# A decoder block on one core: scan factor, value sums and gates moved to other PSUM banks, and the orders of all engines laid anew

## What is computed

```
h = layer_norm(layernorm(x)); xk, xv, xr = mixes of h and h one token earlier
k, v = xk @ Wk.T, xv @ Wv.T;  sr = sigmoid(xr @ Wr.T)
r = sr * wkv(decay, first, k, v)        # a scan over the tokens, with a running maximum
n = layernorm(x); y = n + r @ Wo.T; h2 = layer_norm(y); xk, xr = mixes of h2
x = x + (y + sigmoid(xr @ Wrec.T) * (square(relu(xk @ Wkey.T)) @ Wval.T))
q = layernorm(x); per token: 16 heads of 16, scores q.k / 4 over the 16 heads of the
    same token of ctx, causal mask, softmax, sum over ctx's heads
x = x + that
x = x + gelu(layernorm(x) @ U1 @ V1 + b1) @ U2 @ V2 + b2
```

## Time and profile before

| | us |
|---|---|
| runs of the kernel | 1248.64, 1262.07, 1250.37; median 1250.37 |
| the profiled execution | 1249.77 |
| its span (first to last instruction) | 1247.8 |
| mean granted TensorE clock | 0.945 of full |
| busy: PE, DVE, ACT, POOL | 1032.6, 1111.0, 935.8, 867.1 |

### The profile page before, as it was taken

How to read it: one execution, slowest core, us unless ns; L and a number is a source line. 1 busy time by engine, 2 the same in 40 slices (tenths; PEclk the granted TensorE clock), 3 DMA queues, 4 the chain that set the end, 5 groups by cost and what they waited for, 6 DMA issues and landing times.

```text
span 1247.8 us, 14567 instructions
## 1 busy us (share of the span) xinstructions
PE 1032.6 (83%) x3584; PEld 584.6 (47%) x3584; DVE 1111.0 (89%) x2172; ACT 935.8 (75%) x2005; POOL 867.1 (69%) x783
## 2 busy tenths in 40 slices
PE   2679598989898989989798989989698998869515
PEld 1336263636455463736355463736346363626202
DVE  3755999999999999999999999999999999988681
ACT  4877779698888889796788879697688979464413
POOL 0112968788795968687595968688496968777680
PEclk9789799999999999999899999999899999979657
DMA  5010101001010101010010102001010101010000
GB/s 186 17 51 18 34 1 34 18 18 51 17 51 18 51 17 50 0 48 20 17 50 18 51 0 68 0 18 50 17 50 17 34 1 51 1 34 18 1 17 17
DMA packets 38964, 38.39 MB, mean 31 GB/s; under 512 B 2932, under 2 KB 38648, under 8 KB 38904
## 3 DMA queue, kind: packets, MB, share of 16 engines
q1 hardware_dynamic: 38904, 37.77, 9.5%
HBM read 29.38 MB, written 8.39 MB: 30 GB/s over the span
## 4 chain that ended last, share of the span: by engine, by line
PE 44%; DVE 32%; ACT 11%; issue 7%; POOL 4%; SPq 1%; DMA 0%; DVEq 0%; ACTq 0%; POOLq 0%
PE bank L813 19%; PE bank L870 8%; DVE x L1364 6%; PE bank L901 5%; DVE stat L1154 4%; PE bank L820 4%; PE bank L894 3%; DVE aa L1265 3%; PE bank L913 2%; DVE pp L1222 2%; POOL prod L338 2%; PE bank L885 2%; POOL prod L350 2%; DVE x L1306 2%; ACT n L462 2%
## 5 line engine op out<-in xcount | busy, mean ns | idle before, releaser
L338 POOL TENSOR_TENSOR prod<-q,kv_ctx 128x256 f32<-128x256 f32 (+5 forms) x448 | 394.7, 920 | 221.1 <-ACT q L462 221.1
L350 POOL TENSOR_TENSOR prod<-prob,v_dh 128x256 f32<-128x256 f32 (+3 forms) x256 | 390.9, 1568 | 29.2 <-ACT prob L564 29.2
L813 PE MATMUL bank<-xk,w_key 128*128 128x512 f32 x512 | 241.8, 612 | 17.6 <-DVE xk L1196 17.6
L870 PE MATMUL bank<-w_val,hidden 128*128 128x256 f32 x1024 | 225.9, 379 | 0.0
L870 PEld LDWEIGHTS bank<-w_val,hidden 128*128 128x128 f32 x1024 | 193.6, 190 | 32.4 <-issue 7.7
L1364 DVE TENSOR_REDUCE x<-prod 128x64 f32<-128x256 f32 (+3 forms) x256 | 189.9, 808 | 5.5 <-POOL prod L350 5.5
L1326 DVE TENSOR_REDUCE score<-prod 128x16 f32<-128x256 f32 (+5 forms) x448 | 175.5, 463 | 10.0 <-POOL prod L338 10.0
L813 PEld LDWEIGHTS bank<-xk,w_key 128*128 128x128 f32 x512 | 94.5, 194 | 141.8 <-issue 127.4
L548 ACT ACTIVATE hidden<-bank 128x512 f32<-128x512 f32 x128 | 74.9, 585 | 66.8 <-PE bank L813 66.7
L827 PE MATMUL bank<-ident,n 128*128 128x128 f32 x384 | 61.7, 297 | 75.5 <-ACT n L462 75.5
L422 ACT ACTIVATE lnv<-mv,eps_col 128x4 f32<-128x4 f32 x64 | 18.4, 287 | 127.2 <-DVE mv L1161 127.2
(11 more groups left out here) (96 smaller groups left out, 1946.4 us busy)
## 6 DMA issues: line engine op xcount, KB each, us to landing
x_in<-in_x SPq DMA_DIRECT2D x16, 512.0 KB, 3.6
kv_ctx<-in_ctx SPq DMA_DIRECT2D x16, 512.0 KB, 3.7
n<-in_x SPq DMA_DIRECT2D x16, 512.0 KB, 3.5
out<-y_out SPq DMA_DIRECT2D x16, 512.0 KB, 4.5
w_key<-in_wkey SPq DMA_DIRECT2D x1, 1024.0 KB
w_val<-in_wval SPq DMA_DIRECT2D x1, 1024.0 KB
w_k<-in_wk SPq DMA_DIRECT2D x1, 256.0 KB, 3.8
w_v<-in_wv SPq DMA_DIRECT2D x1, 256.0 KB, 4.2
```

The lines of the kernel that those rows point to most:

```text
L338: ins = pool.tensor_tensor(o, a, b, ALU.mult)
L350: ins = pool.tensor_tensor(o, ph[:, HB * n:HB * n + HB, 0:keys].unsqueeze(2).to_broadcast(shape), vh[:, :, 0:keys].unsqueeze(1).to_broadca ...
L813: mm = pe.matmul(to[:, :], w[:, fi, P * f:P * f + P], src[:, fi, :], start=(fi == 0), stop=(fi == CH - 1))
L870: mm = pe.matmul(bank[6 + t // 2][:, C * (t % 2):C * (t % 2) + C], hidden[:, j, P * t:P * t + P], w_val[:, j, :], start=(j == 0), stop=(j ...
```

## The change

1. The factor e1 isn't a tile any more: `split_rise` and `exp_e1` write it into bank f over k, and both scans read it there. So `project_r(f)`, whose output goes to bank f, waits for `aa_done` of half 0 and `bb_done` of half 1.
2. `sum_values` writes bank 5, `over_mass` works in bank 5, `third_residual` reads bank 5 and writes x3. The two halves s share the bank: `sum_values` for t = 0 waits for x3 of the group before, for t = 2 for the first half's x3.
3. `project_rec`, `gate_of_rec`, `transpose_4` and `copy_n4T` use bank 4 for both halves, one after the other.
4. `ln_den` takes ln(2 den) and `inverse_den` drops its bias operand. `vec` is loaded ahead of `x`.
5. Every engine's list is written anew; the boundary between steps has moved (what was at a step's end is at the start of the next), so numbers of lags differ without more groups being in flight. GpSimd's instructions are the same.

```diff
             def split_rise(g, f):
                 act.wait_ge(rise_done, upto(g, 2, f + 1))
-                act.activation(e1[:, f, :], rr[:, f, :], ACT.Relu)
+                act.activation(bank[f][:, :], rr[:, f, :], ACT.Relu)
...
-                act.activation(e1[:, f, :], e1[:, f, :], ACT.Exp, scale=-1.0).then_inc(e1_exp, 1)
+                act.activation(bank[f][:, :], bank[f][:, :], ACT.Exp, scale=-1.0).then_inc(e1_exp, 1)
...
-                act.activation(rr[:, f, :], rr[:, f, :], ACT.Ln).then_inc(den_ln, 1)
+                act.activation(rr[:, f, :], rr[:, f, :], ACT.Ln, scale=2.0).then_inc(den_ln, 1)
...
-                act.activation(rr[:, f, :], rr[:, f, :], ACT.Exp, scale=-1.0, bias=nln2_col[:, :])\
-                    .then_inc(den_inv, 1)
+                act.activation(rr[:, f, :], rr[:, f, :], ACT.Exp, scale=-1.0).then_inc(den_inv, 1)
...
-                act.activation(pair(gate_rec, s), bank[4 + s][:, :], ACT.Tanh, scale=0.5).then_inc(rec_gate, 1)
+                act.activation(pair(gate_rec, s), bank[4][:, :], ACT.Tanh, scale=0.5).then_inc(rec_gate, 1)
...
-                token_major(bank[4 + s], s, xr, w_rec, rec_mm)
+                token_major(bank[4], s, xr, w_rec, rec_mm)
...
-                transposes(bank[4 + f], f, n4, tr4_mm)
+                transposes(bank[4], f, n4, tr4_mm)
...
                 if on(1):
-                    pe.wait_ge(rise_done, upto(i - 1, 2, 1))
+                    pe.wait_ge(aa_done, upto(i - 1, 2, 1))
                     project_r(i - 1, 0)
                 if on(1):
-                    pe.wait_ge(rise_done, upto(i - 1, 2))
+                    pe.wait_ge(bb_done, upto(i - 1, 2))
                     project_r(i - 1, 1)
...
-                    ins = dve.tensor_tensor_scan(bb[:, SEQ * f + s, 1:T + 1], e1[:, f, cols],
+                    ins = dve.tensor_tensor_scan(bb[:, SEQ * f + s, 1:T + 1], bank[f][:, cols],
...
-                    ins = dve.tensor_tensor_scan(aa[:, SEQ * f + s, 1:T + 1], e1[:, f, cols],
+                    ins = dve.tensor_tensor_scan(aa[:, SEQ * f + s, 1:T + 1], bank[f][:, cols],
...
+                if t == 0 and some(g):
+                    dve.wait_ge(x3_done, upto(g - 1, 2))
+                if t == 2:
+                    dve.wait_ge(x3_done, upto(g, 2, 1))
                 for n, keys, at in V_PARTS:
                     src = prod[slot][:, at:at + HB * HD * keys].rearrange("p (a b) -> p a b", b=keys)
-                    o = heads(par, NH * t + HB * n, NH * t + HB * n + HB).rearrange("p h d -> p (h d)")
-                    ins = dve.tensor_reduce(o, src, AX.X, ALU.add)
+                    row = C * (t % 2) + HB * HD * n
+                    ins = dve.tensor_reduce(bank[5][:, row:row + HB * HD], src, AX.X, ALU.add)
...
-                dve.tensor_tensor(pair(x3[par], s), pair(x3[par], s), pair(x2[par], s), ALU.add).then_inc(x3_done, 1)
+                dve.tensor_tensor(pair(x3[par], s), bank[5][:, :], pair(x2[par], s), ALU.add).then_inc(x3_done, 1)
```

More of the change, by code:

```diff
@@ L717, in step @@
                     relu(i - 2, 1)
-                if on(0):
-                    normalise_1(i, p)
-                if on(2):
-                    square(i - 2, 0)
-                    square(i - 2, 1)
+                if on(1):
+                    ln_den(i - 1, 0)
+                if on(4):
+                    copy_qT(i - 4)
+                if on(1):
+                    inverse_den(i - 1, 0)
                 if on(2):
@@ L921, in step @@
                     project_o(i - 2, 0)
+                if on(1):
+                    pe.wait_ge(xr_done, upto(i - 1, 2, 1))
+                    project_v(i - 1, 0)
                 if on(2):
@@ L1386, in step @@
                 if on(2):
+                    divide_num(i - 2, 0)
+                if on(4):
+                    sum_values(i - 4, 0, 1)
+                    sum_values(i - 4, 1, 2)
+                    over_mass(i - 4, 0)
+                    third_residual(i - 4, p, 0)
+                    sum_mass(i - 4, 1)
+                    inverse_mass(i - 4, 1)
+                    stats_4(i - 4, p, 0)
+                    sum_values(i - 4, 2, 0)
+                if on(1):
+                    att_before_k(i - 1, 0)
+                    att_before_k(i - 1, 1)
+                    att_before_v(i - 1, 0)
@@ new lines, in step @@
+                if on(3):
+                    gate_values(i - 3, 0)
+                if on(1):
+                    att_before_v(i - 1, 1)
+                if on(3):
+                    second_residual(i - 3, 1 - p, 0)
+                if on(4):
+                    sum_values(i - 4, 3, 1)
+                if on(3):
+                    stats_3(i - 3, 1 - p, 0)
+                if on(1):
+                    scan_pp(i - 1, 0)
+                if on(4):
+                    over_mass(i - 4, 1)
@@ new lines, in step @@
+                if on(1):
+                    rise(i - 1, 0)
+                if on(4):
+                    third_residual(i - 4, p, 1)
+                if on(3):
+                    gate_values(i - 3, 1)
+                    second_residual(i - 3, 1 - p, 1)
+                    stats_3(i - 3, 1 - p, 1)
+                    mean_3(i - 3)
+                if on(2):
+                    divide_num(i - 2, 1)
+                if on(4):
+                    stats_4(i - 4, p, 1)
+                if on(1):
+                    scan_pp(i - 1, 1)
@@ new lines, in step @@
+                if on(4):
+                    mean_4(i - 4)
+                if on(1):
+                    att_before_r(i - 1, 0)
+                    att_before_r(i - 1, 1)
+                if on(2):
+                    first_residual(i - 2, p, 0)
+                if on(1):
+                    rise(i - 1, 1)
+                if on(2):
+                    stats_2(i - 2, p, 0)
+                if on(1):
+                    scan_bb(i - 1, 0)
+                if on(2):
+                    first_residual(i - 2, p, 1)
@@ L1415, in step @@
                 if on(3):
-                    top_scores(i - 3, 1)
-                    shift_scores(i - 3, 1)
+                    shift_scores(i - 3, 0)
+                    sum_scores(i - 3, 2, 2)
                 if on(2):
```

523 lines of the change are left out of this document (226 added, 297 removed).

## The result

The changed kernel takes 1371.3 us (median of 4 runs, 1366.8 to 1380.6) against 1251.6 us for the kernel before, a ratio of 1.107 with a 95% interval of 1.099 to 1.116. The forecast was 1221 us, with a range of 1184 to 1256: the sign was wrong. The profiled execution has a span of 1378.7 us and a granted clock of 0.913.

What follows compares the result with a forecast made beforehand. It took a loop of VectorE and TensorE together as the bound. From the profiled 1249.8 us, 14 periods x -1.5 (-21), -16 for over_mass holds and +8 for held divisions gave 1221 us, range 1184 to 1256.

Steps and rivals of the forecast that it cites:

- Operands in banks: VectorE's scans, divisions and residuals with one SBUF input get cheaper: at most 81 us of work, 5.1 us per group.
- the rule of the Trainium skill, "VectorE: DVE Perf Modes": 120 fixed cycles for a PSUM source against 58 for SBUF: 65 ns more per moved operation, 29 us in all.
- First and second piece: Gate 0 to u1 was to shorten by 1.5 us per period; from there through the first gelus, 6.15 us as before.
- the 1.2 us for the aa scans: Term of the first piece: what GpSimd costs the four aa half scans on average, taken off VectorE's stretch.
- Third piece: TensorE's stretch from u2 through v1, keys, rec and half of val to the next gate: 34.6 us, unchanged.
- rival C: divide_num(0), first of VectorE's step, held in most groups at 5.5 us each: 1290 us at 14 of 16; chance 13%.
- 0.9 us of gaps before stats_2 and weigh_token: Term of the first piece: VectorE's gaps of 0.44 and 0.47 us there go away.
- Holds of over_mass: over_mass on VectorE can't be held any more: -16 us, from two periods at 6.9 us and the 15th at some 2.
- the 8 us that were added for held divisions: Two to three holds of divide_num(0) beside GpSimd's value products, 5.5 us each less slack: +8 us.

Runs made afterwards that it cites:

- c3: Kernel before with value sums in bank 5, second gates and fourth transposes in bank 4, scan factor from bank 5 (max for product): 1242.4 us, ratio 1.001.
- c2: Changed kernel with the scan factor e1 back in SBUF, all orders and waits kept: 1310.4 us, ratio 1.047.
- e1: d2 with the hardware loop's turn moved ahead of split_rise on ScalarE and ahead of last_residual on VectorE: 1214.3 us, ratio 0.985.
- c1: Changed kernel with GpSimd waiting for its own add_bb ahead of score_products 2 (c1_join): 1264.1 us, ratio 1.011.
- d2: Changed kernel, GpSimd waiting on itself ahead of score products 2, 3 and all value products, stats_1 and mean_1 behind last_residual: 1249.7 us, ratio 0.998.
- d3: Changed kernel with only stats_1 and mean_1 moved behind last_residual, GpSimd's run left unbroken: 1393.6 us, ratio 1.113.

## Why the prediction was wrong

Point by point, by the prediction's steps:

- *Operands in banks*: right. 670, 669 and 688 ns for the 670, 670 and 680 forecast, reduces 815 for 808; the rule of the Trainium skill, "VectorE: DVE Perf Modes", that was weighed there and put aside is not borne out.
- *First and second piece*: right, and a little better. 26.6 to 26.7 us against 27.0, with r(1) waiting for bb as forecast, and 5.6 or 5.7 us for the second piece, where 6.15 was forecast. Of the terms of the first piece only their sum is borne out: the 1.2 us for the aa scans didn't show in c3.
- *Third piece: "the same matmuls in another order: 34.6 us"*: this is the step that failed. Only matmuls were looked at. It took 44 to 49 us. `add_x_again` stands behind `gate_num` in VectorE's list at the head of that piece, ahead of all that the keys need, and the prediction priced it nowhere. It had the row of 12.78 us for one such hold and the rule that a two-input operation is "held until GpSimd pauses". What it did not do was to ask, operation by operation, where the pauses of GpSimd would be in the new order: the pause of 2.95 us ahead of `add_aa` goes as soon as weigh_bonus comes before the score products end, and the scans that broke the run went to banks. Either alone leaves the way open (c2, c3). It looked for the risk at `divide_num` alone (rival C: 14 holds of 5.5 us); there 7 of 32 took over 2 us and none over 5.
- *"0.9 us of gaps before stats_2 and weigh_token"* were put down as saved. The 0.44 us by issue ahead of `stats_2` was the loop's turn on VectorE; it didn't go but moved, to where it costs 2.3 to 2.9 us, and ScalarE's turn, hidden before in a wait for VectorE of 4.5 us, went to relu 3. The diff said that the boundary between steps moved; that was read as a matter of lags.
- *Holds of over_mass*: gone, as forecast, in every trace with the sums in bank 5. The end of GpSimd's run at 869.25, on which the prediction's reading of such a hold rests, is that of two `add_bb` behind the value products of the earlier trace rows:

```profile
866.91 2.34 POOL L358 TENSOR_TENSOR rr<-rr,bb 128x512 f32<-128x512 f32 x2
```

- *The forecast itself*: from the changed kernel to e1 the times go 1371, 1264 (the hold gone, c1), 1250 (further pauses and the load's wait moved, d2), 1214 (the turns moved, e1). e1 has periods of 67.2 us and takes 1214.3, where 67.8 and 1221 were forecast for the change as it stands. So three things were left out of the sum: the hold, the larger part by far; the place of the load's wait and the held `shift_scores`, 14 us; and the turns, 35 us, which four periods of 76 instead of 67 us account for. That e1 lies so near to the forecast is in part luck: e1 isn't the changed kernel, the 8 us that were added for held divisions were not needed, and against the kernel before in its own set it gains 1.5%, where 2.3% was forecast.

Not settled: why the price of a turn varies (some 1.8 us a round in the changed kernel's trace, 8 to 9 in d2's), why moving the load's wait made d3 slower, and why a held add gets in ahead of the eleventh product in some groups and only at the run's end in others.

## What to carry to other kernels

When an operation with two SBUF inputs runs beside a busy GpSimd, look at how long GpSimd will have been running without a pause when it arrives: each pause and each port user that an edit removes may have been what let it in, and one wait of GpSimd on its own last result gives the way back. The place where a hardware loop turns round is part of the schedule: put it where the engine waits anyway, and look for idle time that comes once a round, by issue or not. A piece of the loop "with the same matmuls" is only the same if what feeds them was priced too.

## What the runs showed of the hardware

- A VectorE operation with two SBUF inputs can be held through 10 to 14 GpSimd instructions, 10 to 12 us. In the changed kernel it ended 1.82 us ahead of the end of GpSimd's run in 9 groups and 1.07 us behind that end in 6. The Trainium skill, "SBUF — State Buffer", section "SBUF: two separate sides", speaks of a lock that whoever starts first holds for its whole instruction; below 8 us of undisturbed run the traces agree (1024 of 1026 got in within one instruction), beyond 12 us they mostly don't (29 of 116).
- A gap of 0.15 us between two GpSimd instructions is enough to be let in (c1_join). Why the way in closes with time was only counted here, not explained.
- Without a wait of its engine or queued work to cover it, the turn of a hardware loop left an engine idle for 2.7 to 2.9 us (VectorE) and 3.2 to 4.1 us (ScalarE) in d2; at the place that it had on VectorE in the kernel before it was 0.4 to 0.8 us. That queued work covers it is an inference from these places.
